# A graph network in four layers: table loads moved from the end of a unit to behind its steps

## The reference

```python
h = relu(layernorm(x))   # before each of the four
# layer 0, 50000 edges
msg = relu(h[src] + edge_attr_16 @ We + be)
x = x + gelu((h + segment_sum(msg, dst)) @ W1 + b1) @ W2 + b2
# layer 1: ten propagation steps with normalised edge weights, self loops included
for _ in range(10):
    h = 0.9 * segment_sum(h[s] * wn[:, None], d) + 0.1 * feat_0
# layer 2: three attention layers over the edges, layer 3: one edge layer with silu
```

## Time and profile before

| | us |
|---|---|
| median of three timed runs | 4477.23 |
| profiled execution | 4463.81 |
| its span, first to last instruction | 4462.0 |
| TensorE matmuls busy | 3304.3 (74%) |
| VectorE busy | 2860.9 (64%) |
| GpSimd busy | 2893.0 (65%) |
| ScalarE busy | 847.1 (19%) |

### The profile page before, as it was taken

How to read it: one execution, slowest core, us unless ns; L and a number is a source line. 1 busy time by engine, 2 the same in 40 slices (tenths; PEclk the granted TensorE clock), 3 DMA queues, 4 the chain that set the end, 5 groups by cost and what they waited for, 6 DMA issues and landing times.

```text
span 4462.0 us, 80494 instructions
## 1 busy us (share of the span) xinstructions
PE 3304.3 (74%) x20313; PEld 2353.7 (53%) x20314; DVE 2860.9 (64%) x10303; ACT 847.1 (19%) x2207; POOL 2893.0 (65%) x3059
## 2 busy tenths in 40 slices
PE   1269417777777999999688786887868788566666
PEld 1269305555554344444466665666656666445554
DVE  6987428878875111111688887888878888755554
ACT  0000002222221000000122222222213222121211
POOL 2677766555557888850277774777747777467776
PEclk9999959899998999999899997999969999755555
DMA  4320013333338999999322223222232222211112
GB/s 142 110 45 10 17 59 89 83 81 87 87 80 262 364 353 364 355 366 353 124 63 62 62 62 51 64 62 62 61 52 62 62 63 61 35 32 28 28 28 30
DMA packets 296076, 497.76 MB, mean 112 GB/s; under 512 B 166412, under 2 KB 211341, under 8 KB 294475
## 3 DMA queue, kind: packets, MB, share of 16 engines
q1 hardware_dynamic: 120919, 340.03, 21.6%
q0 software_dynamic: 92160, 115.39, 13.4%
q10 hardware_dynamic: 82800, 40.01, 3.1%
HBM read 435.66 MB, written 59.08 MB: 111 GB/s over the span
## 4 chain that ended last, share of the span: by engine, by line
PE 31%; POOL 24%; issue 19%; DMA 15%; DVE 9%; DVEq 1%; SPq 1%; ACT 0%; POOLq 0%; ACTq 0%
PE ps L1591 28%; POOL arena L838 16%; DMA arena<-table,arena 12%; POOL rows_dst L821 7%; DMA rows_dst<-stage,arena 1%; DVE arena L1197 1%; DVE arena L1198 1%; PE ps L1777 1%; DMA arena<-in_edge_attr_dram 1%; DMA arena<-dense 1%; DVE arena L1216 1%; DVEq L565 1%; DVE arena L1368 1%; DVE arena L1212 1%; PE ps L1697 1%
## 5 line engine op out<-in xcount | busy, mean ns | idle before, releaser
L838 POOL DMA_INDIRECT arena<-table,arena x2080 | 1983.7, 954 | 1209.3 <-issue 537.3
L1591 PE MATMUL ps<-arena 128*128 128x96 f32 (+6 forms) x9740 | 1644.2, 347 | 579.5 <-DVE arena L1216 240.8
L1591 PEld LDWEIGHTS ps<-arena 128*128 128x128 f32 (+5 forms) x9740 | 1302.2, 227 | 910.6 <-issue 646.7
L1591 PE MATMUL ps<-arena,nodes 125*64 125x500 f32 (+2 forms) x3144 | 652.4, 538 | 35.0 <-DMA arena<-dense 24.4
L1198 DVE TENSOR_SCALAR arena<-iota_row_b,arena 128x128 f32<-128x128 bf16 x2080 | 585.8, 300 | 0.0
L792 POOL DMA_INDIRECT rows_src<-stage,stage_at x400 | 476.2, 1190 | 116.6 <-issue 109.6
L821 POOL DMA_INDIRECT rows_dst<-stage,arena x400 | 402.7, 1007 | 224.2 <-issue 123.0
L1210 DVE TENSOR_TENSOR arena<-ps,arena 128x256 f32<-128x256 f32 x416 | 176.5, 424 | 522.2 <-DMA arena<-table,arena 506.2
L1197 DVE TENSOR_SCALAR arena<-iota_row_b,arena 128x128 bf16<-128x128 bf16 x1664 | 459.3, 278 | 3.0 <-PE ps L1591 0.7
L1591 PEld LDWEIGHTS ps<-arena,nodes 125*64 125x64 f32 (+1 forms) x3144 | 244.6, 137 | 353.1 <-issue 323.6
L1300 DVE TENSOR_TENSOR nodes<-nodes,ps 125x256 f32 (+1 forms) x70 | 27.5, 393 | 610.3 <-PE ps L1777 610.3
(11 more groups left out here) (290 smaller groups left out, 3264.9 us busy)
## 6 DMA issues: line engine op xcount, KB each, us to landing
arena<-dense SPq DMA_DIRECT2D x240, 750.0 KB, 6.6
nodes<-dense SPq DMA_DIRECT2D x60, 750.0 KB
dense<-arena ACTq DMA_DIRECT2D x150, 250.0 KB
arena<-table,arena POOLq DMA_INDIRECT x2080
arena<-dense SPq DMA_DIRECT2D x60, 500.0 KB, 7.6
arena<-rows_dst SPq DMA_DIRECT2D x208, 96.0 KB
arena<-dense SPq DMA_DIRECT2D x6, 2000.0 KB, 21.5
arena<-pair_rows SPq DMA_DIRECT2D x12, 976.6 KB
```

The lines of the kernel that those rows point to most:

```text
L838: nc.gpsimd.indirect_dma_start(rows[:, u, k, 0:width], None, frm, bass.IndirectOffsetOnAxis(ap=p[:, c, j, c_other:c_other + 1].bitcast(I32 ...
L1591: return nc.tensor.matmul(to, lhsT, rhs, start=start, stop=stop, skip_group_check=True)
```

## The change

fetch gets a third argument, after. It counts the loads of a call in the order in which they would be made (four by four, in each the two tables), and with after given it makes only the load with that number. TensorE's dense_steps calls it behind each step k of a unit with after = k, and no longer once behind the last step. The loads of the next unit are the same, four or two; they now stand behind the first four or two steps of this unit, one behind each. Behind the other steps the call makes no load. Unit 0's own fetch at the start of the body and VectorE's fetch give no after and stay as they are. The tables, the steps, their waits and their operands are unchanged.

```diff
--- before.py
+++ after.py
@@ -582,14 +582,19 @@
 
             held_values = {}
 
-            def fetch(i, u):
+            def fetch(i, u, after=None):
+
                 lo_, hi_ = first_step(u) // 4, (first_step(u) + PER_U[u % 2] - 1) // 4
+                n = 0
                 for q in range(lo_, hi_ + 1):
                     if u == 0 or q > (first_step(u) - 1) // 4:
                         for name, (table_, lowest, highest) in tables.items():
-                            values = load_values(eng, table_[0:1, bass.ds(i * PER_BODY + 4 * q, 4)], lowest, highest)
-                            for k in range(4):
-                                held_values[name, 4 * q + k] = values[k]
+                            if after is None or n == after:
+                                values = load_values(eng, table_[0:1, bass.ds(i * PER_BODY + 4 * q, 4)], lowest, highest)
+                                for k in range(4):
+                                    held_values[name, 4 * q + k] = values[k]
+                            n += 1
+                assert n <= min(PER_U)
             return held_values, fetch
 
         def over_units(ops, turn):
@@ -1671,8 +1676,8 @@
                     pe.wait_ge(op_ready, i * PER_BODY + (first + k + 1))
                     mm(flat[:, bass.ds(step_at["bank", first + k], SBW)], lhs[:, slot, :], rhs[:, slot, :],
                        start=False, stop=False).then_inc(built, 1)
-                if u + 1 < U:
-                    fetch_steps(i, u + 1)
+                    if u + 1 < U:
+                        fetch_steps(i, u + 1, k)
 
             def clear(ep):
```

## The result

The kernel after takes 4450.90 us (median of four runs, 4444.64 to 4452.86) against 4477.95 for the kernel before beside it (four runs, 4475.84 to 4479.48).

The account below looks back on a forecast made before the run. TensorE's instruction queue was taken to bound the first pass. Bank waits 11.9, less 1.0 for lost cover, plus 2 in unit 0 gave 13 us, from the median 4477.23 to 4464 us; range 4453 to 4479.

Parts of the forecast that it names:

- The mechanism: TensorE, first pass: its instruction queue's serial work sets the unit; a load costs 0.45 us unless the queue waits there anyway.
- the rival that loads vanish: Moved loads in the first pass hide under matmuls: 134 us less, 4343 us; chance 0.03.
- The thinned stream: Rival, first pass: loads between steps thin TensorE's work and its clock falls; ten such units give 4499 us; chance 0.08.
- The fourteen waits: Waits for a PSUM bank ahead of first-pass step matmuls; loads placed between steps were to cover 11.9 us of them.
- the rival of no change: Where the array lags, the bank's release moves with the loads; only five small waits go: 4 us, 4473 us; chance 0.23.
- the most that could be gained: Upper bound in the first pass: all fourteen bank waits (18 us) and unit 0's 7 us go, 25 us.
- Where it waits anyway: Step that sought first-pass waits in gaps ahead of step matmuls: fourteen bank waits; the other 90 of 104 units gain zero.
- Waits that the fetch at the end used to cover: Short banks across a unit's end lose the cover of the loads there: two remainders of 0.5 us, minus 1.0 us.
- unit 0's, whose term: Unit 0 of each of 13 bodies, where VectorE is barely ahead: loads between steps hide 0 to 7 us, 2 taken.

Follow-up runs that it names:

- The doubled loads: Kernel after, moved loads of the eviction-count table made twice and both used, 156 loads more: 4514.33 us, ratio 1.0087.
- second traces: Kernels before and after each run and profiled once more, unedited: before 4475.22 us (ratio 1.0001), after 4446.96 us (ratio 0.9942).
- first pair: First profiled executions of the kernels before and after: 4463.81 and 4452.24 us, with timed medians of 4477.95 and 4450.90 us.

## Why the prediction was wrong

**The mechanism held.** The queue's serial work sets the unit, loads are paid where they stand (0.436 us measured, 0.43 to 0.45 put) and the plain unit is unchanged (6.59 and 6.55 us). The doubled loads refute the rival that loads vanish. The thinned stream did not let the clock fall more often: time at half clock went from 88.7 to 71.7 us (109.2 to 71.7 in the second traces, from 700 us to the last transpose). It gathered in the units with unit 0's fetch (23.9 to 59.5 us) and nearly left the others (64.8 to 12.2, and 84.4 to 20.2 in the second traces).

**The fourteen waits held in their sum.** On the queue they are 23.1 us before and 10.6 after, 12.5 covered, 22.1 and 9.7 in the second traces, 12.4 covered; the term said 11.9. That the sums agree so well is partly luck. The wait in unit 1 of body 6, put to go (bodies and units count from 0), stayed at 1.03 and 1.09 us, and the one in unit 5 of the same body, put to lose 0.90, grew from 1.50 to 2.09; the second trace of after has 1.08 and 2.10. Ahead of both, in after, the array was at half clock for 3.4 to 4.3 of 6 us, which fits the rival of no change (where the array lags, the release moves with the steps). Another, put at 0.90, gave 2.48. Their total was put at 18, by array gaps and too small, and the range rests on it: with 23.1 in its place the most that could be gained is 30 us, not 25, and the measured 27 lie within.

**The step that failed is "Where it waits anyway".** It looked for waits in the gaps ahead of step matmuls, that is on the array, after it had shown that the queue is what counts, and put every unit without such a gap at zero. The account finds nine more waits of over 0.15 us in the trace of before, 6.3 us in all, and in the second trace twelve, 10.6 us. Most stand ahead of a unit's last step, and all but the first, in body 0, left no gap that the array's timeline shows. One unit before (busy by engine), TensorE in it, and ScalarE:

```profile
1184.35:1192.22 7.87, 6.37 (x25) 5.13 (x26) 6.83 (x27) 2.31 (x4) 6.04 (x7) 0.78 0.33 63
```

```profile
1185.11 5.61 PE L1591 MATMUL ps<-arena 128*128 128x96 f32 x22
```

```profile
1188.12 0.58 ACT L1473 COPY arena<-ps 128x500 f32<-128x500 f32 x1 [5.73 <-PE ps L1591]
1188.73 0.58 ACT L1475 COPY ps<-zeros 128x500 f32<-128x500 f32 x1
```

The clock is 0.78 and the array has a backlog: 22 matmuls run on end, and a reader of the array sees no wait. The queue stood still for 0.96 us all the same, from 1188.3 on, until the clear had ended at 1189.31, and the four loads behind it started that much later. The backlog is also what made the wait: the queue had issued the step that closes the bank by 1185.9, but its matmuls ended on the array at 1188.01, just ahead of ScalarE's copy. The unit lasted 7.87 us. In after the loads come first, the clock is 1.00, and the bank is free when the last step is reached:

```profile
1172.04:1178.92 6.88, 5.78 (x27) 3.40 (x25) 6.83 (x28) 1.16 (x3) 4.87 (x6) 1.00 0.44 99
```

So the term "Waits that the fetch at the end used to cover" had the wrong sign. New waits did come, one of 0.64 us for two of 0.5 put; but 5.1 us of waits that were not on the list went. Together these others went from 6.3 to 1.8 us, and from 10.6 to 1.4 in the second traces: 4.5 to 9.2 us of gain where 1.0 us of loss was put.

What took them away is the loads' new place or the clock, and the runs separate the two only in part. In the traces of before, 3.4 of the 6.3 us and 7.3 of the 10.6 have 2 us or more of half clock in the 4 us ahead of them, the others none. One and the same unit has a wait of 0.06 us ahead of its last step at full clock, in the first trace of before, and of 1.10 in the second:

```profile
1171.46:1177.46 6.00, 5.08 (x25) 3.33 (x26) 5.97 (x24) 3.46 (x6) 4.48 (x6) 1.00 0.49 109
1181.06:1188.06 7.00, 6.51 (x25) 5.08 (x26) 6.96 (x28) 3.08 (x6) 5.33 (x6) 0.76 0.43 97
```

Four of these units ran at full clock in one of the two traces, and there none had a wait over 0.11 us. In after half clock has all but left these units, so that their waits would have gone by that alone. But the waits without half clock ahead went too, all but one in body 0: 2.1 and 1.9 us, for which the loads alone are left. And with the loads behind the last four steps, three units that have waits of 0.65 to 1.99 us in the traces of before at a clock of 0.66 to 0.78 ran at 0.74 to 0.76: in two there was no wait, in the third 0.63 us. So loads ahead of the last step cover such waits, in part at least, at a lowered clock too; how much of the 4.5 to 9.2 us the clock gave stays open. Of the fourteen waits 18.1 us are left in that run.

**What else the sum held and lacked.** In the first pair: waits under 0.15 us 1.5, operand waits 2.5, loads 2.9, less 2.3 in all else. With 12.5 and 4.5 that is 21.6, for 21.5 measured on the queue. What the operand waits lost is nearly all unit 0's, whose term of 2 was about right: in the eleven bodies of the loop they went there from 3.9 to 1.6 us on the queue, and from 4.6 to 1.3 in the second traces. From transpose to transpose, on the array, unit 0 shows none of it (2.7 us more in one pair of traces, 1.4 less in the other). The loads take 0.441 us each instead of 0.447: 64 of them take over 0.6 us, where it was 69 (73 in the second trace); what makes a load long, no run tells.

**The execution that was read.** It was 13 us under the median. The prediction subtracted from the median, which was right, but took the waits from a trace that held fewer: 34.4 us against 37.8 in the next. Of the 27 us between the medians, the passes show 21.2 and 27.0; whether the first pair's trace of before or chance makes the last 6 us is open.

## What to carry to other kernels

Find out first whether an engine's array or its instruction queue sets the pace, and then read all waits there: a wait that the array's backlog hides on the timeline still delays everything queued behind it, and the backlog itself makes such waits, since it holds up the step that a release waits for. Instructions that must be issued somewhere belong between the step that starts a release and the step that needs it. And read two executions before a sum of small waits: here one differed from the next by 4.5 us in the pass alone.

## What the runs showed that I had not expected

- TensorE at half its clock for 58 to 61 us more of a pass (129.7 and 133.1 us against 71.7) cost nothing on the queue but what its waits and loads account for. It is not free: some of those waits come of the array's backlog at half clock.
- An eviction copy does not shrink in proportion to its columns: 128x500 took 0.57 to 0.58 us, 128x8 0.17.
- A check of a semaphore against a register is 0.242 us of queue at the least (0.093 + 0.149). Dropping 303 of them gained 34 us in the order of before (ratio 0.9924) and 23 to 25 in that of after (0.9886 against 0.9938 and 0.9942), about as much as the change itself.
